# A transformer block in one core: first half of batch 1's v ahead of unit 0, shared relu ahead of a table load, first down in unit 6, q parts stored ahead of the second maxima

## What is computed

```python
xn = _layernorm(x, axis=-1)
x = x + attn(xn, Wq, Wk, Wv) + ffn(xn, gate_w, e_bias, up_w, down_w, shared_up_w, shared_down_w)

# attn, per batch and head
scores = jnp.einsum('bhqd,bhkd->bhqk', q, k) / np.sqrt(HEAD_DIM)
out = jnp.einsum('bhqk,bhkd->bhqd', jax.nn.softmax(scores, axis=-1), v)

# ffn: 4 of 8 groups, then 6 of 32 experts for each token
scores = jax.nn.sigmoid(x @ gate_w.T)
h = _relu2(jnp.einsum('th,eih->tei', x, up_w)) * combine[:, :, None]
moe_out = jnp.einsum('tei,ehi->th', h, down_w)
shared = _relu2(x @ shared_up_w.T) @ shared_down_w.T
```

## Time and profile before

| | us |
|---|---|
| median of 3 runs | 613.78 (613.65 to 613.85) |
| the profiled execution | 609.7 |
| its span, first to last instruction | 607.9 |
| PE busy | 600.1 (99%) |
| DVE busy | 429.4 (71%) |
| ACT busy | 404.0 (66%) |
| POOL busy | 427.7 (70%) |

### The profile page before, as it was taken

How to read it: one execution, slowest core, us unless ns; L and a number is a source line. 1 busy time by engine, 2 the same in 40 slices (tenths; PEclk the granted TensorE clock), 3 DMA queues, 4 the chain that set the end, 5 groups by cost and what they waited for, 6 DMA issues and landing times.

```text
span 607.9 us, 20120 instructions
## 1 busy us (share of the span) xinstructions
PE 600.1 (99%) x8237; PEld 266.7 (44%) x8237; DVE 429.4 (71%) x1066; ACT 404.0 (66%) x795; POOL 427.7 (70%) x512
## 2 busy tenths in 40 slices
PE   8999999999999999999999999999999999999997
PEld 6432544444444444434444434444443443444343
DVE  7899975777767777677867778586766878666402
ACT  4578667766776666766666676666667665666663
POOL 6850478677796778867788678877776766667653
PEclk9999999999999999999999999999999999999999
DMA  5168744646436254652438454263545633343430
GB/s 150 35 202 217 167 108 100 208 105 158 111 90 210 61 150 110 214 138 71 122 78 243 106 158 109 65 210 81 141 112 174 177 77 99 82 103 72 106 72 18
DMA packets 56252, 76.19 MB, mean 125 GB/s; under 512 B 10464, under 2 KB 23648, under 8 KB 56160
## 3 DMA queue, kind: packets, MB, share of 16 engines
q1 hardware_dynamic: 56140, 74.90, 46.0%
q10 hardware_dynamic: 20, 0.00, 0.0%
HBM read 56.14 MB, written 18.35 MB: 123 GB/s over the span
## 4 chain that ended last, share of the span: by engine, by line
PE 92%; DVE 4%; POOL 2%; issue 1%; DMA 0%; ACT 0%; POOLq 0%; DVEq 0%
PE acc L1053 21%; PE pv L1211 20%; PE st L1053 14%; PE upb L1053 10%; PE st L1181 9%; PE sc L1170 6%; PE upb L1181 4%; PE st L1186 3%; DVE nmax L923 2%; PE upb L1186 1%; PE st L1153 1%; POOL g L553 1%; PE upb L1088 1%; PE upb L1153 1%; DMA gate_at<-in_x 0%
## 5 line engine op out<-in xcount | busy, mean ns | idle before, releaser
L923 DVE TENSOR_REDUCE nmax<-sc 128x1 f32<-128x512 f32 x512 | 328.0, 685 | 136.9 <-PE sc L1170 126.7
L693 ACT ACTIVATE probs<-st 128x512 f32<-128x512 f32 x364 | 205.3, 595 | 32.0 <-PE st L1186 27.1
L556 POOL TENSOR_TENSOR gated<-gate_at,relu 128x512 f32<-128x512 f32 x111 | 141.9, 1279 | 97.3 <-ACT relu L698 93.3
L560 POOL TENSOR_TENSOR g<-gated,relu 128x512 f32<-128x512 f32 x111 | 142.2, 1281 | 16.2 <-POOL gated L556 0.4
L1186 PE MATMUL st<-stacks 32*128 32x512 f32 x364 | 148.6, 578 | 0.0
L1211 PE MATMUL pv<-probs,v_aug 128*32 128x512 f32 x1024 | 136.4, 605 | 0.1
L1170 PE MATMUL sc<-stacks 32*128 32x512 f32 x512 | 134.3, 493 | 1.3 <-DVE nmax L923 1.0
L1053 PE MATMUL acc<-dn,g 128*32 128x128 f32 x3512 | 135.0, 274 | 0.2
L1053 PEld LDWEIGHTS acc<-dn,g 128*32 128x32 f32 x3512 | 112.1, 114 | 23.7 <-issue 22.8
L693 ACT ACTIVATE probs<-upb 128x512 f32<-128x512 f32 x148 | 88.0, 595 | 19.2 <-PE st L1186 14.1
L1181 PE MATMUL st<-m_rows,ones 3*128 3x512 bf16 x364 | 99.0, 385 | 0.3 <-ACT sh L680 0.3
(11 more groups left out here) (178 smaller groups left out, 554.0 us busy)
## 6 DMA issues: line engine op xcount, KB each, us to landing
gate_at<-gate_rows SPq DMA_DIRECT2D x62, 512.0 KB, 6.3
stacks<-q_stack SPq DMA_DIRECT2D x30, 256.0 KB, 6.7
stacks<-k_stack SPq DMA_DIRECT2D x30, 256.0 KB, 6.8
q_stack<-qk_parts SPq DMA_DIRECT2D x28, 256.0 KB, 6.4
k_stack<-qk_parts SPq DMA_DIRECT2D x28, 256.0 KB, 5.7
x_res<-in_x SPq DMA_DIRECT2D x8, 256.0 KB, 7.7
out<-y SPq DMA_DIRECT2D x8, 256.0 KB, 7.1
m_rows<-m_parts SPq DMA_DIRECT2D x95, 4.0 KB
```

Source lines behind the costliest of these rows:

```text
L556: nc.gpsimd.tensor_tensor(gated[:, u % 2, :], gate_at[:, group % RING, u % GATES, :], relu[:, u % RELUS, :], ALU.mult).then_inc(gated_read ...
L560: nc.gpsimd.tensor_tensor(g[:, u % 2, :], gated[:, u % 2, :], relu[:, u % RELUS, :], ALU.mult).then_inc(g_ready, 1)
L693: nc.scalar.activation(probs[:, u % 2, h, :], ring_b("st", u * QUAD + h)[:], ACT.Exp).then_inc(probs_ready, 1)
L923: nc.vector.tensor_reduce(out=nmax[:, s % 2, at:at + 1], in_=sc_b[tile % SC_BANKS][:], op=ALU.max, axis=AXX, negate=True).then_inc(s_read, 1)
```

## The change

It has five parts. (1) The first half of batch 1's v is made ahead of unit 0's first couple, in place of after it; in the ring it becomes the first use, so v takes `st0` and the first couple `st1` and `upb`. (2) ACT's `shared_relu(0, 0)` is done ahead of the table load for the exponential. (3) The first down, with the wait for the down weights, stands in unit 6 (`FIRST_DOWN`); the shared downs stay in unit 7. (4) The units with two downs become 8, 10, 12 and 14. (5) SP stores the four q parts of batch 1 ahead of `load_max(1)`, and the k parts after it.

```diff
-LAG, FIRST_LAG = 2, 7
+LAG, FIRST_LAG, FIRST_DOWN = 2, 7, 6
-TWO_DOWN = (9, 11, 12, 13, 15)
+TWO_DOWN = (8, 10, 12, 14)
@@ place_downs
-    for u in range(FIRST_LAG, UNITS):
+    for u in range(FIRST_DOWN, UNITS):
@@ build
-        OUT_ORDER = BESIDE + (("v", 0), ("x", 1), ("max", 0), ("shared", 0)) + BEHIND
+        OUT_ORDER = BESIDE + (("v", 0), ("x", 1), ("max", 0)) + BEHIND
@@ ring_order
+                if u == 0:
+                    order = [("v", 0)] + [use for use in order if use != ("v", 0)]
@@ block.sync, main loop
+                    if s == 0:
+                        store_rows(1, 0, slice(0, H), stored)
                     load_max(s + 1)
                     if s == 0:
-                        store_parts(1)
+                        store_rows(1, 1, slice(0, H), stored)
                         load_x(FIRST_X)
@@ block.scalar, after the maxima's own DMA
+                    shared_relu(0, 0)
                     act.wait_ge(sigmoid_set, 1)
                     nc.scalar.activation(blank_out[:], blank[:, 0:1], ACT.Exp).then_inc(exp_set, 1)
@@ block.tensor
-                if v_made(u):
+                if u and v_made(u):
                     make_half(*v_made(u))
+            make_half(*v_made(0))
             for u in range(UNITS):
-                if u == FIRST_LAG:
+                if u == FIRST_DOWN:
                     pe.wait_ge(dn_ld, NDN * 16)
```

More of the change, by code:

```diff
@@ L741, in _ @@
                     v_out(i)
-                elif kind == "shared":
-                    shared_relu(0, i)
                 elif kind == "x":
```

## The result

| | before | after |
|---|---|---|
| median in us (22 runs each) | 613.70 (609.21 to 618.70) | 614.79 (613.82 to 616.38) |
| the profiled execution, us | 609.7 | 615.11 |
| its span, us | 607.9 | 613.3 |
| its mean granted clock of PE | 1.000 | 0.994 |

The ratio after to before is 1.0036, 95% interval 1.0020 to 1.0052: 2.2 us slower (1.2 to 3.2). The forecast was 5.1 us slower. The two profiled executions differ by 5.4.

A forecast was written before the change was run, and what follows sets the result against it. TensorE (PE) was taken to bound the kernel, 92% of the chain that ended last. The terms 0 + 2.9 + 3.1 - 0.9 gave +5.1 us, median 613.8 to 618.9, range 616.8 to 621.5.

The forecast's parts named there:

- The sum is made on the profiled execution and carried to the median as a difference.: Whole kernel: the sum on the profiled 609.7 us moves the median, 613.78, by the same difference; the gap is 4.1.
- the first wait: At unit 4 PE waits for the second maxima, put at 2.9 us.
- the forecast's 3.5 to 7: Ends of the sum: 2.5 at unit 4 and a quicker gate load, +3.5; 3.5 there and 1 us contention, +7.
- First half of v and relu, 0: Around unit 0: PE gains up to 0.29 us but keeps none; value 0, ends -0.3 and +0.3.
- q stores, a wait of 2.9 at unit 4: Unit 4: q stores ahead of the maxima make PE wait 2.9 us, between 2.5 and 3.5.
- First down at 63.5, PE 6.0 us behind: Unit 6: the down waits for g until 63.5 instead of 57.48; 6.0 us lost, 2.9 at unit 4, 3.1 here.
- The steps of its chain: From routing to the first down: transposed gates 52.9, gate load issued about 56.9, g 63.4, down 63.5.
- Recovered, 0.9: After the first down: PE, now later than its suppliers, loses its small waits; 0.9 us back, between 0.3 and 1.1.
- The named waits of before: PE's small waits that go away: 0.8 us for g over three waits between 60 and 100, 0.3 for DVE.
- A microsecond before unit 17 is one at the end: Before unit 17: each microsecond PE waits is one at the end, since no other engine sets the pace later.
- The clock falls, chance 0.12: Rival: behind two waits of about 3 us, one or two falls, 1.5 us each; 620.4 to 621.9, chance 0.12.
- Not slower: Rival at unit 6: g ready by 57.5 instead of 62.3, 612.6 or less; chance 0.08 within 0.2%, 0.05 faster.

The follow-up runs named there:

- late_dn_route: `route_late` with SP issuing q stores, maxima and k stores ahead of the down weights, residual and next x behind the gates; 609.32 us, 0.9942.
- q_route: `route_late` with the four q stores ahead of the second maxima; 611.90 us, 0.9985.
- undo_down: The changed kernel with the first down back in unit 7 and the old list of units with two downs; 614.31 us, 1.0028.
- after_again: The changed kernel once more, unchanged, on one chip beside the kernel before; 614.85 us, 1.0035.
- v_relu: The kernel before with only the first half of v and the shared relu moved; 612.88 us, 1.0004.
- best: `late_dn_route` with the first half of v ahead of unit 0 and the relu ahead of the table load; 609.45 us, 0.9942.
- q_only: The kernel before with only the four q stores ahead of the second maxima; 615.04 us, 1.0037.
- route_late: The kernel before with DVE's routing of batch 1 one unit later and nothing else changed; 608.99 us, 0.9938.
- base: The kernel before, unchanged, run against itself; 613.7 us, 1.0018.

## Why the prediction was right or wrong

**The step that failed** is the one at the start: "The sum is made on the profiled execution and carried to the median as a difference." On the profiled execution the total holds, +5.1 forecast and +5.4 found, in part by luck: the first wait was 0.85 us shorter than its term, two falls of the clock, put at nothing in the sum, cost 1.65 and 1.5, and 2.2 came back in place of 0.9. But the median of before, 4.1 us above it, was not the same run plus a constant. Three runs of four had a mean clock of 0.998 or less, so falls that the profiled one did not have, and by the profiles of the neighbouring kernels pauses too; the new waits partly take their place. With the routing moved a unit later on both sides, the change costs 5.8 us, within the forecast's 3.5 to 7; on the kernel as it was, 2.2. The hint was there: 4.1 us between the median of the runs and the profiled time, beside a clock of exactly 1.000. The prediction named the gap and didn't ask what filled it.

That the changed kernel no longer pays for the place of that routing is shown by the pair of runs: the same edit gains 3.8 us by the ratio, 4.4 by the medians, on before and none on after. That it is the collision, and how, is read from the traces: PE now stands still for g in unit 6, DVE's routing is held from 62.35 on, partly in that time, and no wait of PE for DVE follows in unit 7. In the trace of after, timeline of DVE:

```profile
62.35 1.23 DVE L866 TENSOR_TENSOR sc<-sig,ebias 128x128 f32<-128x128 f32 x1
63.61 1.17 DVE L868 TENSOR_TENSOR pair<-sc 128x32 f32<-128x32 f32 x1
```

This reading is from profiles alone; the runs don't separate the collision from other effects of later routing.

Point by point:

- *First half of v and relu, 0.* Nothing speaks against it. 1.0004 alone, and 609.45 against 609.32 on top of `late_dn_route`, are too coarse for 0.3 us, but in the traces PE starts the second couple of unit 1 at 35.69 before and 35.74 after.
- *q stores, a wait of 2.9 at unit 4.* The mechanism is right, the size high: 2.05 in the profiled run, 1.54 in the second one of the same kernel, 1.42, 0.37, 1.77 and 1.42 in the other kernels that have the edit and keep the down weights ahead of it. SP came to the q stores at 41.07 and not 42.75, because its long load issue took 3.37 and not 4.53, and the maxima went out at 44.26 and not 45.3. The fall of the clock added 1.65, of which some tenths came back by the end of unit 6: PE was 3.4 behind there (60.84 against 57.48), where 2.9 had been put down.
- *First down at 63.5, PE 6.0 us behind.* Right: 63.53, 6.05 behind. The time held although the first wait was off, as the prediction had said. The steps of its chain were each off by some tenths and made up for one another: gates at 52.30 (52.9), their load issued at 56.16 (56.9), g begun at 62.17 (62.1).
- *Recovered, 0.9.* Too small. PE was 6.05 behind at the first down, lost 1.5 more to the second fall and was 5.39 behind at unit 17 (120.35 against 114.96) and 5.4 at the end: 2.2 came back. The named waits of before explain 1.1; the rest isn't assigned.
- *A microsecond before unit 17 is one at the end.* Right: 5.39 and 5.4. And since 1.42 us in `q_route` vanished before unit 17, the small waits up to there are worth less than their length.
- *The clock falls, chance 0.12.* Far too low. All 34 runs of the changed kernel have a mean clock under 0.998. Its price, 1.5 for a fall, was about right (1.65 and 1.5). In the total a larger recovery covers it. The Trainium skill's rule is that an idle array goes back to half rate (TensorE: Matmul & The Clock Gate, section What's actually happening). The trace agrees in kind: the waits of 2.05 and 2.69 us were both followed by a clock of 0.50.
- *Not slower.* It did not happen, as judged: the first down waits 3.36 and 3.51 us even where the q stores stand behind the maxima.

## What to carry to other kernels

Before a sum is carried from a profiled execution to the median, compare the two, in time and in mean clock: a gap of several microseconds and a clock of 1.000 meant here that the profile showed the less common, short run, and what lengthens the usual run can absorb the cost of a change or be absorbed by it. Where PE sets the pace, price a wait near 2 us as the wait and a fall of the clock together, and keep DVE's two-input operations that stand ahead of anything PE needs out of the time in which POOL starts a burst. Costs of two waits on one chain need not add up, since the later can cover part of the earlier: here 2.9 and 4.0 to 4.9 alone gave 5.8 together, which the noise leaves open.

## What of the hardware was unexpected

- **A short pause is enough for the clock.** PE waits of 1.77, 1.98, 2.05, 2.10, 2.15, 2.16, 2.69, 3.05, 3.36 and 3.51 us were each followed by windows at or near 0.50; those of 1.42, 1.42 and 1.54 in `undo_down`, `q_route` and `after_again` were not, but one of 1.62 in `v_relu` was, and one of 0.92 in `best`. So the length of the pause alone does not decide. Nor is the price fixed: by the windows (twice the missing share of the clock) the stretch at the lower level was some 3 us behind each wait of the changed kernel, some 7 behind the waits for DVE in `undo_down` and `q_only`, and about 10 behind the late stack in `route_late`, whose span of 612.4 is 5.2 above its median.
- **DVE held by POOL.** A 128 by 32 operation with two inputs in SBUF took 1.1 to 1.3 us instead of 0.2 beside a 1.27 us POOL multiplication, in the profiles of `v_relu`, `base`, before and after.
- **The same issue varies.** SP's issue of the residual took 4.53 us in the profiled run of before and 3.37, 3.35, 3.21 and 2.50 in those of after, `undo_down`, `v_relu` and `q_only`. It alone can move the maxima by up to 2 us.
